# Experts of a four-layer kernel: shared expert as a list of 64 units, routing for two groups of tokens at once

## The reference, cut to what matters

```
scores = softmax(x @ gate_w.T);  s = scores + gate_b      # 16 experts in 4 groups
keep the 2 groups with the largest sum of their two best s; take the 2 best experts in them
y = sum over the 2 experts e of scores[e] * ((silu(x@We1[e]+be1[e]) * (x@We3[e]+be3[e])) @ We2[e] + be2[e])
z = (silu(x@ws1+bs1) * (x@ws3+bs3)) @ ws2 + bs2           # shared expert, hidden size 256
return y + z
```

## Time and profile before

| | us |
|---|---|
| median of 3 runs | 3576.29 (3575.45 to 3598.54) |
| span of the profiled execution | 3535.8 |
| median less that span: what lies around it | 40.5 |
| TensorE busy in the span | 3212.6 (91%) |
| VectorE busy | 2704.2 (76%) |
| ScalarE busy | 2334.4 (66%) |
| GpSimd busy | 1781.8 (50%) |

### The profile page before, as it was taken

How to read it: one execution, slowest core, us unless ns; L and a number is a source line. 1 busy time by engine, 2 the same in 40 slices (tenths; PEclk the granted TensorE clock), 3 DMA queues, 4 the chain that set the end, 5 groups by cost and what they waited for, 6 DMA issues and landing times. The chain is left out here.

```text
span 3535.8 us, 116953 instructions
## 1 busy us (share of the span) xinstructions
PE 3212.6 (91%) x46878; PEld 2155.6 (61%) x46878; DVE 2704.2 (76%) x5988; ACT 2334.4 (66%) x4989; POOL 1781.8 (50%) x3252
## 2 busy tenths in 40 slices
PE   8989899999999999999999989999779969969960
PEld 6766455555555555555555547888657656648860
DVE  7867899999999999999999954666535437855658
ACT  5555587787788777877887775777534536635533
POOL 1441377777777777777777672111000004646761
PEclk9999899999999999999999999999979989989985
DMA  7697533333333333333333312221051123336667
GB/s 242 222 261 233 90 85 84 79 81 84 82 79 82 84 81 79 83 85 79 80 84 86 75 51 93 79 90 67 25 175 48 48 73 125 116 132 184 190 203 268
DMA packets 380531, 396.76 MB, mean 112 GB/s; under 512 B 121368, under 2 KB 294424, under 8 KB 377816
## 3 DMA queue, kind: packets, MB, share of 16 engines
q1 hardware_dynamic: 366264, 351.46, 35.8%
q0 software_dynamic: 13728, 37.83, 2.9%
HBM read 230.29 MB, written 157.25 MB: 110 GB/s over the span
## 5 line engine op out<-in xcount | busy, mean ns | idle before, releaser
L809 ACT ACTIVATE att_p<-att_st 128x512 f32<-128x512 f32 (+3 forms) x3072 | 1328.4, 492 | 391.8 <-PE att_st L715 360.7
L895 DVE TENSOR_REDUCE att_mcol<-att_ring 128x1 f32<-128x512 f32 (+1 forms) x2048 | 1235.6, 650 | 125.1 <-PE att_ring L715 117.3
L715 PE MATMUL att_st<-att_ops_more 99*32 99x512 bf16 (+3 forms) x9216 | 681.2, 326 | 6.6 <-DMA att_ops_more<-att_mpart 4.8
L715 PE MATMUL att_ring<-att_ops_more 96*32 96x512 bf16 (+3 forms) x9216 | 650.8, 328 | 2.0 <-DMA att_va_more<-values 1.2
L881 POOL TENSOR_SCALAR_AFFINE_SELECT att_p<-att_p 128x512 f32<-128x512 f32 x512 | 324.2, 633 | 378.8 <-ACT att_p L809 369.9
L762 PE MATMUL att_pv<-att_p,att_va_more 128*32 128x512 f32 (+3 forms) x4608 | 475.6, 485 | 4.2 <-POOL att_p L881 2.4
L715 PEld LDWEIGHTS att_st<-att_ops_more 99*32 99x32 bf16 x9216 | 249.0, 97 | 291.5 <-ACT att_p L809 111.3
L715 PE MATMUL att_ring<-c_mask,c_identb 128*32 128x128 bf16 x8192 | 413.9, 221 | 0.0
L715 PEld LDWEIGHTS att_ring<-att_ops_more 96*32 96x32 bf16 x9216 | 252.4, 97 | 133.4 <-issue 40.4
L715 PEld LDWEIGHTS att_ring<-c_mask,c_identb 128*32 128x32 bf16 x8192 | 228.3, 98 | 82.0 <-issue 14.5
L715 PE MATMUL att_st<-att_ops 99*32 99x512 bf16 (+3 forms) x3072 | 229.4, 328 | 8.4 <-DMA att_ops<-att_mpart 8.2
(11 more groups left out here) (298 smaller groups left out, 6663.7 us busy)
## 6 DMA issues: line engine op xcount, KB each, us to landing
att_ops_more<-parts SPq DMA_DIRECT2D x1152, 64.0 KB, 3.0
parts<-prj_pt SPq DMA_DIRECT2D x128, 384.0 KB, 3.2
att_ops<-parts SPq DMA_DIRECT2D x384, 64.0 KB, 2.9
moe_work<-moe_rows SPq DMA_DIRECT2D x79, 261.0 KB
values<-prj_vs SPq DMA_DIRECT2D x16, 1024.0 KB, 6.7
heads<-att_ofin SPq DMA_DIRECT2D x128, 128.0 KB, 2.6
ffn_os<-heads SPq DMA_DIRECT2D x16, 1024.0 KB, 4.9
moe_work<-x SPq DMA_DIRECT2D x32, 512.0 KB, 4.3
```

The source lines that it names most:

```text
L715: ins = nc.tensor.matmul(out[row:row + VC], stationary[:, row:row + VC], moving, start=start, stop=stop, tile_position=(0, row))
L809: act.activation(pr[:, g % R, b, off:GN], stp[(t * NST + n) % NS][:, off:GN], ACT.Exp, scale=SCALE).then_inc(exp_done, 1)
L895: ins = v.tensor_reduce(to[:, h, c, i % HB if c else i:(i % HB if c else i) + 1], of[:, 0:w], AX.X, ALU.max)
```

## The change

- The shared expert becomes a list `SHARED` of 64 units: 32 halves of a hidden layer and 32 halves of a down product. In the middle they alternate. Each engine walks the same list, and the routing's pieces are tied to positions in it: `route_at(g)` = 13g//4 - 4 for the transposes of group g (one half of the channels there, the other at the next position, the logits at the one after), and `CHAIN_AT[q]` = 2, 8, 15, 21, 28, 34, 41, 47 for the vector pieces of pair q.
- `shift`, `group_scores`, `two_groups`, `two_experts`, `slots` and `counts` work on a pair of groups (QT = 8 tiles) at once. On TensorE the counts of pair q stand behind the unit at `CHAIN_AT[q] + 2`.
- The vector steps that work out the tile tables are cut in three pieces at positions 50, 51 and 52. SyncE writes the paddings when the counts are known (`rows_ready` 3), and loads expert tiles as soon as the tables are there; the first `turn` stands ahead of the last two units.
- All 16 groups of the input are loaded at the start into `moe_sh`, where the shared result will go, and so are the transposed copies kept. `xn` has five buffers. ScalarE writes the second normalised set by a copy of the first. One PSUM bank for transposes and one for the down product, where there were two for both together.

```diff
+SHARED = [("hidden", 0, 0), ("hidden", 0, 1)]
+for _g in range(G):
+    for _n in range(2):
+        SHARED += [("hidden", _g + 1, _n)] * (_g + 1 < G) + [("down", _g, _n)]
+
+def route_at(g):
+    return 13 * g // 4 - 4
...
-    XN, YB, XR = 4, 5, 7
+    XN, YB, XR = 5, 5, 7
+    QT = 2 * GT
+    NQ = G // 2
+    CHAIN_AT = [route_at(2 * q + 1) + 3 for q in range(NQ)]
+    TABLES_AT = CHAIN_AT[-1] + 3
...
-        xs, xn = first.take("r t e", r=2, t=GT, e=E), first.take("r k t e", r=XN, k=2, t=GT, e=RW)
+        xn = first.take("r k t e", r=XN, k=2, t=GT, e=RW)
+        xs, xt = sh, sh[:].rearrange("p g t e -> p g (t e)").rearrange("p g (c n) -> p g c n", c=EC)
...
@@ TensorE
+            for k in range(route_at(0), len(SHARED)):
+                if k == len(SHARED) - 2:
+                    pe.wait_ge(rows_ready, 5)
+                    turn(0)
+                if k >= 0:
+                    kind, g, n = SHARED[k]
+                    if kind == "hidden":
+                        hidden(g, n)
+                    else:
+                        down(g, n)
+                for g in range(G):
+                    if k in (route_at(g), route_at(g) + 1):
+                        transposes(g, k - route_at(g))
+                    if k == route_at(g) + 2:
+                        logits(g)
+                for q in range(NQ):
+                    if k == CHAIN_AT[q] + 2:
+                        counts(q)
+                if k == TABLES_AT + 1:
+                    turn_tables()
+            pe.wait_ge(sh_ready, 2 * G)
...
@@ TensorE, down
             def down(g, n):
                 pe.wait_ge(h_done, 2 * g + 2)
+                if g or n:
+                    pe.wait_ge(sh_ready, 2 * g + n)
...
@@ ScalarE
+                for t in range(GT):
+                    ins = act.activation(xn[:, g % XN, 0, t, 0:E], xs[:, g, t], ACT.Identity, ...)
+                ins.then_inc(xn_ready, 1)
+                act.wait_ge(xn_ready, 2 * g + 1)
+                act.activation(xn[:, g % XN, 1, :, 0:E], xn[:, g % XN, 0, :, 0:E], ACT.Copy).then_inc(xn_ready, 1)
...
@@ VectorE
+            for k in range(len(SHARED)):
+                for q in range(NQ):
+                    if k == CHAIN_AT[q]:
+                        shift(q)
+                        if q + 2 < NQ:
+                            scales(q + 2, (q + 2) % 3, QT)
+                        if q + 3 < NQ:
+                            pre_stats(q + 3, 0)
+                        group_scores(q)
+                    if k == CHAIN_AT[q] + 1:
+                        two_groups(q)
+                        if q + 3 < NQ:
+                            pre_stats(q + 3, 1)
+                    if k == CHAIN_AT[q] + 2:
+                        two_experts(q)
+                    if k == CHAIN_AT[q] + 3:
+                        slots(q)
+                if k == TABLES_AT:
+                    tile_counts()
+                if k == TABLES_AT + 1:
+                    tile_tables()
+                if k == TABLES_AT + 2:
+                    keep_tables()
+                kind, g, n = SHARED[k]
+                if kind == "hidden":
+                    gate(g, n)
+                else:
+                    keep(g, n)
...
@@ GpSimd
+            for q in range(NQ):
+                if q + 3 < NQ:
+                    power.serve(nc, pool, var[:], rstd[:, q % 3], q + 3)
+                for h in range(2):
+                    send(2 * q + h)
...
@@ SyncE
-            sp.wait_ge(rows_ready, 5)
+            sp.wait_ge(rows_ready, 3)
             for e in range(NE):
...
+            sp.wait_ge(rows_ready, 5)
             for i in range(NT2):
                 load_tile(i)
                 if i % EVERY == EVERY - 1 and i // EVERY < XR:
+                    if i // EVERY == 0:
+                        sp.wait_ge(sh_ready, 2 * G)
```

More of the change, by code:

```diff
@@ L1769, in experts @@
     RW = GW + 1
-    XN, YB, XR = 4, 5, 7
+    XN, YB, XR = 5, 5, 7
+    QT = 2 * GT
+    NQ = G // 2
+    SENT = [16 * 2 * GT * len(range(r, G, XN)) for r in range(XN)]
+    CHAIN_AT = [route_at(2 * q + 1) + 3 for q in range(NQ)]
+    TABLES_AT = CHAIN_AT[-1] + 3
+    LAST_SILU = SHARED.index(("hidden", G - 1, 1))
     EVERY = NT2 // (XR + 1)
@@ L1818, in experts @@
         steps, tile_no = m.sb("steps", [P, B * S // TT]), m.sb("tile_no", [P, 1])
-        n_of, over = m.sb("n_of", [P, NE]), hh[:, 0].rearrange("p (e n) -> p e n", e=NE)
+        n_of, over = m.sb("n_of", [P, NE]), first.take("e n", e=NE, n=B * S // TT)
         tri, ends, starts = m.sb("tri", [P, NE, NE]), m.sb("ends", [P, NE]), m.sb("starts", [P, NE])
@@ L2015, in _ @@
-            pe.wait_ge(consts, NC)
-            transposes(0)
-            logits(0)
-            for g in range(G):
-                hidden(g, 0)
-                if g + 1 < G:
-                    transposes(g + 1)
-                hidden(g, 1)
-                if g + 1 < G:
-                    logits(g + 1)
-                down(g)
-                counts(g)
-            pe.wait_ge(tab_ready, 2)
-            for n in range(2):
-                ins = nc.tensor.matmul(tp[0][0:1, n * P:n * P + NT2], tab[0:NT2, n:n + 1], C["ident"][0:NT2, 0:NT2], start=True, stop=True)
@@ L2031, in _, with turn_tables @@
-            ins.then_inc(tabt_ready, 1)
-            pe.wait_ge(rows_ready, 5)
-            pe.wait_ge(sh_ready, 2 * G)
+                ins.then_inc(y_ready, 1)
+            def turn_tables():
+                pe.wait_ge(tab_ready, 2)
+                for n in range(2):
+                    ins = nc.tensor.matmul(tp[0:1, n * P:n * P + NT2], tab[0:NT2, n:n + 1], C["ident"][0:NT2, 0:NT2], start=True, stop=True)
+                ins.then_inc(tabt_ready, 1)
             def turn(i):
@@ L2066, in outer @@
                 ins.then_inc(yx_ready, 1)
-            turn(0)
+            pe.wait_ge(C["s_moe"], C["n_moe"])
+            pe.wait_ge(consts, NC)
+            for k in range(route_at(0), len(SHARED)):
[8 more added lines that the diff above has]
+                        down(g, n)
+                for g in range(G):
+                    if k in (route_at(g), route_at(g) + 1):
[8 more added lines that the diff above has]
+            pe.wait_ge(sh_ready, 2 * G)
             before = None
@@ new lines, in _, with tile_counts @@
+            n_steps = B * S // TT
+            def tile_counts():
+                v.tensor_copy(pad_i[:], base[0:1]).then_inc(rows_ready, 1)
+                own.link(v.tensor_tensor(n_of[:], base[:], first_row[:], ALU.subtract))
+                own.link(v.tensor_tensor(over[:], bcast(n_of[:].unsqueeze(2), [P, NE, n_steps]), bcast(steps[:].unsqueeze(1), [P, NE, n_steps]), ALU.is_gt))
+                own.link(v.tensor_reduce(n_of[:], over[:], AX.X, ALU.add))
+                own.link(v.tensor_tensor(tri[:], lower[:], bcast(n_of[:].unsqueeze(1), [P, NE, NE]), ALU.mult))
+                own.link(v.tensor_reduce(ends[:], tri[:], AX.X, ALU.add))
@@ L2251, in _ @@
             v.tensor_copy(xw[:, :, BI + 1], C["xb3"][:, 0:NE]).then_inc(rows_ready, 1)
-            pre_stats(0)
-            scales(0, 0)
-            pre_stats(1)
-            scales(1, 1)
-            shift(0)
-            for g in range(G):
-                if g + 2 < G:
-                    pre_stats(g + 2)
-                group_scores(g)
-                gate(g, 0)
-                if g:
-                    slots(g - 1)
-                if g + 2 < G:
-                    scales(g + 2, g % 2)
-                two_groups(g)
-                gate(g, 1)
-                if g + 1 < G:
-                    shift(g + 1)
-                two_experts(g)
-                keep(g)
@@ L2272, in _ @@
-            slots(G - 1)
-            v.tensor_copy(pad_i[:], base[0:1]).then_inc(rows_ready, 1)
-            own.link(v.tensor_tensor(n_of[:], base[:], first_row[:], ALU.subtract))
-            n_steps = B * S // TT
-            own.link(v.tensor_tensor(over[:], bcast(n_of[:].unsqueeze(2), [P, NE, n_steps]), bcast(steps[:].unsqueeze(1), [P, NE, n_steps]), ALU.is_gt))
-            own.link(v.tensor_reduce(n_of[:], over[:], AX.X, ALU.add))
-            own.link(v.tensor_tensor(tri[:], lower[:], bcast(n_of[:].unsqueeze(1), [P, NE, NE]), ALU.mult))
```

296 lines of the change are left out of this document (142 added, 154 removed).

## The result

The changed kernel takes 3634.59 us (median of 4, 3633.17 to 3641.51) beside 3580.52 for the kernel before it (median of 4): a ratio of 1.0156, 95% interval 1.0132 to 1.018. It is 54 us slower, where 5 us were forecast.

What follows compares the result with a forecast made beforehand. TensorE was taken to bound the experts' stage, VectorE almost level. Gains of 38.4 us against additions of 43.7 gave 5 us more than the median 3576.3: 3581 us, range 3554 to 3596.

Steps and rivals of the forecast that it cites:

- (a): TensorE's 34.7 us gap between last down product and first expert matmul goes away: 30.9 us gained.
- rivals 3 and 5: Before expert tile 0: rows late, 3588 us, chance 0.10; or gap stays 30 us and waits add, 3610, chance 0.03.
- (g): New waits of TensorE's counts for VectorE's selection, now one burst per pair: 23.2 us added over eight pairs.
- the walk: Instruction-by-instruction timing from a pair's logits: VectorE's selection takes 13.9 us, 10.15 from pair 5, against TensorE's units meanwhile.
- Rival 1: Selection isn't late at TensorE's counts, so its waits and clock loss vanish: 29 us faster, 3547, chance 0.14.
- (e): Start of the list: statistics of eight tiles before the first scale and a single transpose bank: 2 us added.
- (h): TensorE's clock falls to 1.2 GHz after the new waits, by the skill's throttling rule: 11.2 us, taken as 11.
- (b): TensorE's old waits for the selection in the list, and one before the last down product, go: 5.5 us gained.
- (d) and (f): TensorE's added work: 44 count matmuls a pair instead of 28, 3.3 us; transposes split in two calls, 2 us.
- Rival 2: TensorE's new waits come but its clock doesn't fall: 11 us less, 3570, chance 0.13.
- Rival 4: TensorE's clock doesn't come back between waits, recovery over 12 us: up to 3640, half of them 3610, chance 0.04.
- (i): Tables' product behind unit 51 on TensorE waits for VectorE's tables: 2 us added.

Runs made afterwards that it cites:

- after_paced: Changed kernel with GpSimd's sixteen scatters of a pair spread over six units, two or three to a unit: 3602.5 us, ratio 1.0028 to the kernel before.
- before_again: The kernel before, unchanged, run again for a second trace: 3599.0 us, one run.
- before_paced: Kernel before the change with its eight scatters of a group held back to three, three and two: 3591.0 us, ratio 0.9992.
- best1: Changed kernel with paced scatters, counts and slots one unit later, statistics moved behind slots, counts by 9 matmuls: 3579.9 us, ratio 0.9959 to the kernel before.
- after_stats: Changed kernel with VectorE's two halves of the statistics moved behind slots and a unit later: 3626.5 us, ratio 1.0118 to the kernel before.
- after_plain_back: Changed kernel with the expert tiles' scatters replaced by plain DMAs from the sync engine's queue, outputs in wrong rows: 3647.2 us, ratio 1.0136 to the kernel before.

## Why the prediction was wrong, by its steps

- **(a), the gap gone: right.** Tile 0 follows the last down product by 1.8 us, and rows weren't late (rivals 3 and 5 false in the changed kernel).
- **(g), the new wait: right in place, 4 us small.** 27.3 against 23.2. By pairs 2.7, 6.0, 2.7, 4.7, 1.9, 5.5, 0, 3.6 where 2.5, 4.2, 4.15, 5.85, 2.5, 0.45, 0.4, 3.1 were forecast; in after_paced, nearly undisturbed, 2.7, 4.5, 4.9, 6.2, 4.0, 2.1, 1.5, 3.7. There the first four pairs are within 0.8 us of the walk, the later ones 0.6 to 1.6 us longer. Rival 1 is false.
- **The hand-offs that the sum has at nothing: this step failed, and it is the miss.** Behind its counts the walk lets TensorE run on with no wait for any other engine. Measured are 42.8 us of waits at the copies' bank and the downs' bank. (The signs of being wrong named waits for gates and for rows, neither of which came, and not these two; the single bank had its price only in (e), at the start.) The prediction priced GpSimd's sends only as time on GpSimd (20.3 us a pair, for the rows' arrival) and as free to everyone else. They hold up TensorE's signals, and it is their unbroken length that the change doubled. In the profile of before nothing showed it. With the scatters spread the change costs 1.0028, 10 us (1.0007 to 1.0049: 3 to 18), close to the 5 forecast, but in part by luck: there the clock still costs 7 more than (h) and the selection 5 more than (g), and against that the kernel before had 13.8 us of waits to lose where (b) says 5.5.
- **(h), the clock: too small by more than half.** Of the changed list TensorE is busy for 83.9 us at the lower level (granted clock 0.50); half of that, 42 us, is an estimate of the price. before_again has 33.1, so 17, and the first profile, from which the prediction worked, 12.9, so 6. The change adds 25 us by the one and 35 by the other, where 11.2 were forecast. In after_paced it still adds 18 (69.9, so 35). Without these halves the changed list and before_again's hold the same work, 218.5 and 218.9 us, so nothing shows of the 5.3 of (d) and (f). Four of the low stretches are 13.7 to 17.1 us long. Three of them, nearly in full (us, TensorE busy, granted clock, DMA share, GB/s):

```profile
3115.50:3129.00 13.50, 6.70 (x61) 0.50 0.03 11
3149.70:3166.60 16.90, 13.95 (x78) 0.50 0.03 9
3183.80:3197.30 13.50, 8.91 (x57) 0.50 0.08 28
```

  The rule quoted with (h) held in its sign: longer waits, more work at 1.2 GHz. Rival 2 is false, the clock fell. Rival 4 is true in part: it asked for a recovery of over 12 us, and these stretches are that long, but TensorE waits for up to half of them, and the clock came back in between (a mean of 0.86 in the stretch from 3100). That 3634.6 lies between its two numbers is no proof of it: after_paced has three stretches of over 10 us too and takes 3602.5.
- **(e) right:** 12.0 us from the first load to the first transposes, 9.6 before: 2.4 for 2. **(i)** measured 0.7 to 1.2 for 2. **(b)** was 5.5; in before_again TensorE's waits for gates in the list came to 13.8, so the change had more to gain there than was claimed.
- **The base: wrong.** One profiled execution was taken as typical, and the 40.5 us that it lacked as overhead. They went with late signals: 28 us in its list and 42 in its tiles, less the 10 by which its earlier stages were longer. That number was the warning that the trace left something out.

## What to carry to other kernels

Merging two rounds of work into one halves the fixed costs, but it also makes one long stretch out of two on every queue it uses: look at the DMA issues too, and spread indirect DMAs between the units they run beside. Then look in the trace whether they are: a wait for a unit that is long over spreads nothing, as in before_paced and best1. Where a wait is taken away and turns up unchanged at the next hand-off, the banks aren't the cause; look for the signal that all of them wait for, and compare when it was due with what another engine was doing. And a profile whose span is 1% under the runs' median is not the execution that the median measures.

## What the runs showed of the hardware

- While GpSimd issues indirect DMAs back to back (0.96 us each, 1.27 apart), TensorE's signals reach ScalarE and VectorE late in this kernel: by 2 us or less in the first 7 us of a stretch that is not paced, then up to 4 us in one of 8 scatters and up to 9 to 11, with some edits 13, in one of 16; some 3 us behind the end the held-up signals are through. VectorE's signal to ScalarE, shift to exponentials, is not late: 0.03 us in all eight pairs. In the bursts of 44 count matmuls TensorE itself is stopped between matmuls that wait for nothing, with starts 0.7, 1.4 or 2.1 us apart (after_stats).
- Two scatters for each 3.4 us tile are enough for it (37 late silus of 79); without them 3 are. One execution of the kernel before, with all its scatters, had none of it, and no run says why.
- The Trainium skill ("SBUF — State Buffer", "Who interferes with whom") has it that "DMA never contends with a compute engine" but for GpSimd's own descriptor writing being starved. That is said of the memory's ports; what was measured here is that GpSimd's DMAs cost TensorE time all the same, by late signals, and no run shows whether a port has a part in it. Where the sentence is read as saying that a DMA can't slow an engine, the measurement decides.
- The first profile differs from all the others in one more thing. Each scatter steps its semaphore 16 times, 2048 in all for the list. Its trace has 2024 of these steps, before_again's 781, the changed kernel's 586, after_paced's 1122. In stretches of 50 us from 2950 to 3400 it has 698 to 989 semaphore records of all kinds, before_again 287 to 414; after_plain_back has 743 to 876 from 3250 to 3500, where its scatters and its lateness are gone.
- The Trainium skill ("NOTIFIC — the notification-queue block", section 3, "Interfaces") says that back-pressure from the block that writes trace records, when a queue of it is full in one of its modes or an internal one fills, is what can stall an engine. Missing records and late signals together would fit; against it, after_paced misses records too (287 to 407 in 50 us of its list) and is hardly late there. No run here shows such a queue, nor whether the lateness exists with no profiler attached. How the scatters do it stays open.
